# One more source block by matmul in 32, one-hots made ahead of the scans, and span places read from PSUM, in a four-layer graph network

## What is computed

```
L0: segment_sum(relu([h[dst], h[src], ea32] @ W1 + b1) @ W2 + b2, dst)
L1: a = softmax of edge_weight1 over the edges of one dst
    elu(segment_sum(h[src] * a, dst))
L2: segment_max((h[dst] - h[src]) @ theta_w.T + theta_b + (h @ phi_w.T + phi_b)[src], dst)
L3: x + segment_sum(MLP([h[src], h[dst], ea16]), dst) / max(count, 1)
```

## Time and profile before

| | |
|---|---|
| median of 3 runs | 7607.3 us (7605.17 to 7608.85) |
| profiled execution | 7605.69 us, of which 7603.9 us are the span |
| granted TensorE clock | 0.941 of full speed over the span |
| busy: PE / PEld | 6502.0 us (86%) / 5106.3 us (67%) |
| busy: DVE / ACT / POOL | 5489.6 us (72%) / 2251.9 us (30%) / 5677.8 us (75%) |
| indirect gathers | 2770 in layers 0 and 3, 2497 in layers 1 and 2 |
| layer 1 / layer 2, first to last gather | 2146.56 to 3702.18 us / 3860.03 to 5425.34 us |

### The profile page before, as it was taken

How to read it: one execution, slowest core, us unless ns; L and a number is a source line. 1 busy time by engine, 2 the same in 40 slices (tenths; PEclk the granted TensorE clock), 3 DMA queues, 4 the chain that set the end, 5 groups by cost and what they waited for, 6 DMA issues and landing times.

```text
span 7603.9 us, 89481 instructions
## 1 busy us (share of the span) xinstructions
PE 6502.0 (86%) x30127; PEld 5106.3 (67%) x30127; DVE 5489.6 (72%) x6578; ACT 2251.9 (30%) x5060; POOL 5677.8 (75%) x5964
## 2 busy tenths in 40 slices
PE   0799999999689999999579999999409999999995
PEld 0577777777577777777457777777306777776674
DVE  6588888888667777777777777777647777777773
ACT  5144444444222222222310000000005555555552
POOL 7777777777777777777767777777777777777776
PEclk9999999999789999999779999999759999999996
DMA  8366666666433433433223333333215555555553
GB/s 328 93 168 156 154 157 156 155 156 156 113 73 81 86 81 83 85 83 84 62 58 75 75 75 75 74 76 75 54 40 131 145 142 143 143 144 142 145 142 83
DMA packets 1081140, 864.83 MB, mean 114 GB/s; under 512 B 583026, under 2 KB 884820, under 8 KB 1080564
## 3 DMA queue, kind: packets, MB, share of 16 engines
q1 hardware_dynamic: 872480, 649.12, 29.9%
q0 software_dynamic: 192112, 167.52, 15.4%
q10 hardware_dynamic: 16100, 42.47, 1.4%
HBM read 492.83 MB, written 365.69 MB: 113 GB/s over the span
## 4 chain that ended last, share of the span: by engine, by line
POOL 38%; PE 17%; issue 13%; DVE 3%; DMA 2%; ACT 0%; POOLq 0%; DVEq 0%
POOL G L698 32%; PE pOdd L934 7%; PE pRows L934 4%; POOL R_hidden L719 2%; POOL R L719 2%; PE pEven L1036 2%; DVE onehot L1346 1%; POOL first_rows L659 1%; DMA G<-table,idx 1%; DVE S L1395 1%; PE pT L1022 1%; PE pRows L1055 1%; PE pOdd L1043 1%; PE pEven L1043 1%; PE pOdd L926 0%
## 5 line engine op out<-in xcount | busy, mean ns | idle before, releaser
L698 POOL DMA_INDIRECT G<-table,idx x2770 | 2614.3, 944 | 844.3 <-issue 824.8
L698 POOL DMA_INDIRECT G<-table,e_dst x2497 | 2362.4, 946 | 795.9 <-issue 753.1
L1281 DVE TENSOR_TENSOR_SCAN K<-mask_f,K,pT 48x512 f32<-48x512 bf16 x782 | 1005.3, 1286 | 783.7 <-PE pT L1022 633.0
L934 PE MATMUL pOdd<-h_high,onehot 128*128 128x480 f32 (+1 forms) x3880 | 1518.6, 391 | 0.0
L934 PE MATMUL pOdd<-h_low,onehot 128*128 128x480 f32 (+1 forms) x3880 | 1489.7, 384 | 0.0
L934 PE MATMUL pRows<-h_high,onehot 128*128 128x480 f32 (+1 forms) x2430 | 952.9, 392 | 4.1 <-DVE h_low L1134 4.1
L816 ACT ACTIVATE K<-pT 48x512 f32<-48x512 f32 x782 | 461.1, 590 | 1657.2 <-PE pT L1022 1645.8
L934 PE MATMUL pRows<-h_low,onehot 128*128 128x480 f32 (+1 forms) x2430 | 921.0, 379 | 0.0
L1346 DVE TENSOR_TENSOR onehot<-mask_f,pEven 128x2560 fp32r<-128x2560 f32 (+1 forms) x390 | 891.6, 2287 | 17.1 <-DMA mask_f<-pick_row 17.1
L1022 PE MATMUL pT<-ident,G 128*112 128x128 f32 x3128 | 484.0, 278 | 430.8 <-DMA G<-table,idx 416.2
L934 PEld LDWEIGHTS pOdd<-h_high,onehot 128*128 128x128 f32 x3880 | 749.6, 193 | 128.0 <-issue 3.2
(11 more groups left out here) (213 smaller groups left out, 11392.7 us busy)
## 6 DMA issues: line engine op xcount, KB each, us to landing
prefix<-O_hidden SPq DMA_DIRECT2D x390, 512.0 KB
mask_f<-same_row SPq DMA_DIRECT2D x392, 256.0 KB, 3.4
prefix<-O SPq DMA_DIRECT2D x194, 512.0 KB, 3.7
G<-first_rows SPq DMA_DIRECT2D x784, 96.0 KB
G<-table,idx POOLq DMA_INDIRECT x2770
G<-table,e_dst POOLq DMA_INDIRECT x2497
first_rows<-zeros ACTq DMA_DIRECT2D x14, 2688.0 KB, 16.2
K<-in_ea_dram SPq DMA_DIRECT2D x588, 64.0 KB
```

The source lines that it names most:

```text
L698: pool.indirect_dma_start(rows[:, slot, j, 0:widths[l]], None, table[l], bass.IndirectOffsetOnAxis(ap=at[:, n, j:j + 1], axis=0))\
L934: last = pe.matmul(out[:, 0:(stop - first) * D], rows_of[:, g, :], part[:, first:stop, :].rearrange("p b d -> p (b d)"), start=False, stop ...
L1281: dve.tensor_tensor_scan(K[r, c.slot, :], mask_of(c, r), pT[c.slot % 2][r, :], K[r, (c.slot - 1) % RING, CHUNK - 1:CHUNK], ALU.mult, ALU.add)\
```

## The change

Three things change. The list of picked chunks of layers 1 and 2 takes n % 32 in (4, 12, 28) in place of n % 16 = 12. In the order of layers 1 and 2, `mark_next` stands ahead of `scan_streams`. And the places 0 to 9 of a span are copied into PSUM (`span_place`, in `pT[0]`, which nothing else uses then), and the comparison that makes `unchosen` reads them there.

```
-PICK_EXTRA = RING + 4
+PICK_EXTRA = (4, 12, 28)
...
-    return [n for n in range(chunks) if n % RING in PICK_SLOTS or n % (2 * RING) == PICK_EXTRA]
+    return [n for n in range(chunks) if n % RING in PICK_SLOTS or n % (4 * RING) in PICK_EXTRA]
...
+        span_place = pT[0][:, 0:SPAN]
...
+            link(dve.tensor_copy(span_place, pick_id[:, 0:SPAN]))
             link(dve.tensor_tensor(
                 unchosen[:, :, :], pick_x[:, 1, :].rearrange("p (i o) -> p i o", o=1).to_broadcast([P, NP_ALL, SPAN]),
-                pick_id[:, 0:SPAN].rearrange("p (o s) -> p o s", o=1).to_broadcast([P, NP_ALL, SPAN]), ALU.not_equal,
+                span_place.rearrange("p (o s) -> p o s", o=1).to_broadcast([P, NP_ALL, SPAN]), ALU.not_equal,
                 saturate=False))
...
-                          1: [(2, turn_out), (0, turn_in), (0, place_next), (1, scan_streams), (0, mark_next)],
-                          2: [(2, turn_out), (0, turn_in), (0, place_next), (1, scan_streams), (0, mark_next)],
+                          1: [(2, turn_out), (0, turn_in), (0, place_next), (0, mark_next), (1, scan_streams)],
+                          2: [(2, turn_out), (0, turn_in), (0, place_next), (0, mark_next), (1, scan_streams)],
```

## The result

The changed kernel takes 7569.4 us (median of 4 runs, 7565.1 to 7571.9) against 7607.3 us: ratio 0.9949, 95% interval 0.9937 to 0.9962. The forecast was 7568.6 us, in a range of 7563 to 7582. Its profiled execution took 7569.6 us, of which 7567.5 are the span.

A forecast was written before the change was run, and what follows sets the result against it. POOL's gathers, issued without a hole, were taken to bound layers 1 and 2. From the profiled 7605.7 us, - 32.5 - 6.7 + 0.5 gave 7567.0; with the median 1.6 higher, 7568.6 us, range 7563 to 7582.

The forecast's parts named there:

- The bound: Layers 1 and 2 last as long as POOL's gathers; 26 gathers fewer at 1.2485 us save 32.5 us.
- The scatter: Ahead of layer 0: the scatter beside DVE's comparison takes 0.97 us in place of 7.69, saving 6.7 us.
- The 0.5 us of waiting: Layers 1 and 2: POOL waits 0.5 us in all for later scans; bounds 0 and 3.
- The room at the layers' starts: Scans of duo 0 to duo 4's gathers: 1.3 us left in layer 1, 0.4 in layer 2.
- PE's room: Layers 1 and 2: PE needs 1477 us against POOL's 1541, 64 us short at full clock, 34 at 0.98.
- The pick of 4.475 us: On PE in layers 1 and 2: one pick takes 4.475 us, one matmul that hides and 20 products.
- the group sums: Four duos with picks 1222: PE 31.33 us, POOL 31.21; with 1212: PE 26.85, POOL 32.46.
- The order: Layers 1 and 2: mark ahead of scans removes PE's 1 us stall behind a one-pick duo; by itself saves 0.
- part 1: 13 more picks in each of layers 1 and 2: 26 gathers fewer on POOL, 32.5 us saved.
- Rival (a): Ahead of layer 0: scatter stays long, held for another reason than the second SBUF input; 7575 us, chance 0.08.
- Rival (b): Layers 1 and 2: later scans make POOL wait, costing 12 to 24 us; 7580 to 7593 us, chance 0.11.
- Rival (c): Layers 1 and 2: PE becomes the bound through extra work or a lower clock, taking the 64 us; chance 0.05.

The follow-up runs named there:

- the run that makes PE the bound: Changed kernel with n % 32 = 20 picked as well, mark ahead of the scans: 7555.9 us, ratio 0.9933.
- 27 of 32: Picks at n % 32 in (4, 12, 28), as in the changed kernel; that kernel with the scans ahead of the mark again: 7569.8 us.
- 28 of 32: Changed kernel with n % 32 = 20 picked as well: 7555.9 us with the new order, 7638.1 us with the old one.

## Why the prediction was right

**The bound.** POOL's gathers without a hole set layers 1 and 2 before and after; 26 gathers x 1.2485 us = 32.5. Measured by the layers' first to last gather: 1555.62 - 1539.45 = 16.2 in layer 1, 1565.3 - 1549.3 = 16.0 in layer 2. With the 6.3 us ahead of layer 1 that is 38.5 us, against 38.7 forecast. That the total agrees to 0.8 us (7569.4 and 7568.6) holds some luck: the wait for the last stores, which the sum left alone, differs by up to 4 us between executions.

**The scatter.** Forecast 6.7, measured 6.4 in the scatters' own length of this execution, and 6.8 and 7.0 in the two runs of the places alone. It was all on the path: transposes at 308.3, forecast near 308. This holds for chips on which PE's early picks are done before the scatters; on the slower ones the scatters are off the path by 54 us.

**The 0.5 us of waiting.** The room at the layers' starts was worked out as 1.3 and 0.4 us; in layer 1 it is 0.37, and in layer 2 nothing, with 0.07 us of waiting. The longest wait is at duo 8, which the forecast had not looked at. POOL waits 0.4 us in all. Right in size, and partly luck: with scans 1 us later each layer would have had a hole.

**PE's room.** PE stayed short of POOL (1494 us busy of 1541 in layer 1). The pick of 4.475 us and the group sums held to 0.1% in the run that makes PE the bound, 31.36 against 31.33 us a group.

**The order.** The forecast said that the order by itself saves 0, which the run of the order alone shows; that it gives PE the room "that part 1 uses" is not so at 27 of 32: without it the time is the same. It is so at 28 of 32, by 82 us. This step of the forecast is wrong, and its sum doesn't need it.

**Rival (a)**, the held scatter, falls with the row of 0.96 us. **Rival (b)**, POOL waiting for late scans, doesn't occur on the chip of the forecast, but it is what happens on the slower chips, where it ends 2.3% slower; that a chip may hand PE's sums over 3 to 6 us late was in none of my cases. The forecast is right for chips of the first kind alone. **Rival (c)**, PE as the bound by a lower clock: the granted clock stayed at 0.98 in both layers.

## What to carry to other kernels

When one engine issues without a hole, count its instructions: removing one is worth its start-to-start interval, and a reordering on any other engine is worth nothing until that engine's own sum reaches the same length; then it can be worth more than the work that was moved. Keep account of the room between a release and the instruction that it releases, since a stage put ahead of the release spends it: on the first chip the order spent all of it and cost nothing, on chips where PE's sums come up to 6 us late the same order costs 2.3%. The order that is neutral at the present load (the old one here) is the safer one unless the load is raised to where the new one pays; on the chip of the forecast that version, 28 picks in 32 with the new order, is the fastest at 7555.9 us. It was not run on the slower chips.

## What the runs showed of the hardware

A DVE comparison with two SBUF inputs holds an indirect DMA on POOL to its end (7.69 us and, back to back, 6.92); with one of them in PSUM the DMA takes 0.96 us. The comparison isn't slower for it: 7.19 us for 6750 elements with either place, 7.32 in PSUM and 7.33 in SBUF for 6880. The Trainium skill, "SBUF — State Buffer", section "Who interferes with whom", infers that descriptor generation isn't held by such an instruction. For these scatters the trace shows otherwise. The same section's rule, that two SBUF inputs contend with a GpSimd instruction that reads SBUF, agrees with the trace, as the scatter's row numbers (`first_edge`) lie in SBUF; whether it is their reading or the writing of descriptors that is held, no run here tells.

TensorE's granted clock falls to its lower level (1.2 GHz) for 3.4 or 6.8 us at a time in some executions: between 2200 and 3600 us for 51 us in the kernel before, 44 with the order alone and 34 in the changed kernel, and not once in the changed kernel with the old order or with 28 picks in 32 in either order. A duo with two picks takes 8.8 us on PE from the start of its first matmul to the start of its last, and 10.1 to 11.5 when it meets such a fall.

The same program, the kernel before, takes 7607 us on some chips and 9214 to 9313 us on others. On the latter DVE begins the reduction of PE's sums 4.2 to 6.0 us after the start of the last product (old order), in place of 0.38, and layer 0's first transposes come at 382 to 398 us in place of 308 to 315.
